# GpSimd's order of issue in a mixture-of-experts stage: the scatter of the tile two back ahead of the gather of the tile three ahead

## The reference

```python
# layer 0: 8 experts, top 2, hidden width 512
router_logits = x_flat @ moe_router
topk_logits, topk_idx = jax.lax.top_k(router_logits, 2)
topk_weights = softmax(topk_logits)
...
w13_out = jax.lax.ragged_dot(x_sort, moe_w13, group_sizes)
gate, up = jnp.split(w13_out, [512], axis=-1)
out_dispatch = jax.lax.ragged_dot(silu(gate) * up, moe_w2, group_sizes)
out_flat = zeros.at[token_ids_sort].add(out_dispatch * w_sort[:, None])
...
# layer 1: 16 experts, top 4 (of 2 groups out of 4), hidden width 256
for e in range(E):
    we = jnp.sum(weights * (indices == e), axis=-1)
    h = jax.nn.silu(x2 @ W1[e].T + b1[e]) * (x2 @ W3[e].T + b3[e])
    y = y + (h @ W2[e].T + b2[e]) * we[:, None]
...
# around them
x = x + tanh(g_xattn[0]) * xattn0(layernorm(x), ctx)
x = x + tanh(g_ffn[0])   * ffn0(layernorm(x))
x = x + tanh(g_xattn[1]) * xattn1(ctx, layernorm(x), mask)
x = x + tanh(g_ffn[1])   * ffn1(layernorm(x))
```

## Time and profile before

| | us |
|---|---|
| median of 3 runs | 2451.17 |
| lowest, highest | 2448.51, 2455.49 |
| the profiled execution, whole | 2443.97 |
| its span in the trace | 2442.2 |
| experts of layer 0, first gather to last scatter's start | 847.8 to 1190.0 |
| experts of layer 1, first gather to last scatter's start | 2023.3 to 2436.4 |
| PE busy over the span | 2078.9 (85%) |
| DVE busy | 1352.3 (55%) |
| POOL busy | 1291.8 (53%) |
| ACT busy | 929.8 (38%) |

### The profile page before, as it was taken

The page is one execution under the profiler, slowest core; times in us unless marked ns, Lnnn a source line. Parts: engine busy times, 40 slices in busy tenths (PEclk is TensorE's granted clock), DMA queues, the critical chain, the costliest instruction groups (busy, mean ns, idle before and its releaser), DMA issues. The chain is left out here.

```text
span 2442.2 us, 38632 instructions
## 1 busy us (share of the span) xinstructions
PE 2078.9 (85%) x10678; PEld 1354.3 (55%) x10678; DVE 1352.3 (55%) x4084; ACT 929.8 (38%) x2409; POOL 1291.8 (53%) x1552
## 2 busy tenths in 40 slices
PE   3988888888888499999578888888888857999997
PEld 3666666666666256666335555555555533555554
DVE  3666666666666211212247777777776743555554
ACT  1333333333333122222145655556555522333332
POOL 1333343433333234444247767777775744777777
PEclk9999999999999699999789999999998977999999
DMA  3101101010106022223201011011010535555554
GB/s 116 31 24 34 31 27 32 26 35 23 35 23 225 17 39 45 48 44 48 38 19 32 21 32 32 21 32 29 24 32 21 160 98 130 79 76 78 79 78 73
DMA packets 143793, 127.40 MB, mean 52 GB/s; under 512 B 48505, under 2 KB 134241, under 8 KB 143590
## 3 DMA queue, kind: packets, MB, share of 16 engines
q0 software_dynamic: 39456, 46.11, 11.8%
q1 hardware_dynamic: 96348, 70.67, 10.4%
q10 hardware_dynamic: 7786, 8.14, 1.0%
HBM read 87.16 MB, written 37.65 MB: 51 GB/s over the span
## 5 line engine op out<-in xcount | busy, mean ns | idle before, releaser
L1768 PE MATMUL psG<-expert_w,xgT 128*128 x688 | 329.3, 601 | 2.7 <-ACT xgT L1709 2.0
L549 ACT ACTIVATE prob<-psS,nm 100x361 f32<-100x361 f32 x256 | 141.4, 557 | 427.3 <-DVE nm L632 420.8
L777 POOL TENSOR_SCALAR prob<-prob,rc 100x363 f32<-100x363 f32 x256 | 160.4, 638 | 211.9 <-DVE rc L637 210.7
L1794 PE MATMUL psD<-expert_w,hT 128*128 x916 | 230.5, 384 | 2.8 <-ACT hT L1726 2.8
L1581 POOL DMA_INDIRECT xg<-xn,slots x178 | 175.6, 987 | 98.6 <-issue 50.9
L1594 POOL DMA_INDIRECT out<-y,slots x115 | 185.2, 1611 | 70.4 <-issue 25.9
L1709 ACT ACTIVATE xgT<-psX 128x256 f32<-128x256 f32 x172 | 66.0, 383 | 354.3 <-PE psX L1756 354.3
L1594 POOL DMA_INDIRECT acc<-y,slots x57 | 90.1, 1580 | 172.5 <-DVE y L1675 168.6
L971 PE MATMUL psJ<-wkv,cTn 96*121 96x512 f32 x384 | 181.2, 609 | 0.0
L1794 PEld LDWEIGHTS psD<-expert_w,hT 128*128 128x128 f32 x916 | 160.4, 190 | 21.4 <-issue 4.7
L1768 PEld LDWEIGHTS psG<-expert_w,xgT 128*128 128x128 f32 x688 | 118.8, 193 | 88.5 <-issue 88.5
(11 more groups left out here) (260 smaller groups left out, 4849.4 us busy)
## 6 DMA issues: line engine op xcount, KB each, us to landing
expert_w<-in_L_ffn_moe_w SPq DMA_DIRECT2D x8, 1024.0 KB
xn<-xm SPq DMA_DIRECT2D x64, 100.0 KB
bias<-in_L_ffn_b ACTq DMA_DIRECT2D x3, 2048.0 KB
ctx<-in_ctx SPq DMA_DIRECT2D x32, 181.5 KB
cT<-in_ctxT SPq DMA_DIRECT2D x32, 180.5 KB, 2.9
cT<-in_ctxT SPq DMA_DIRECT2D x64, 90.2 KB, 2.9
expert_w<-in_L_ffn_moe_w SPq DMA_DIRECT2D x8, 512.0 KB
expert_w<-in_L_ffn_W1T SPq DMA_DIRECT2D x16, 256.0 KB
```

The costliest lines, as they stand in the source:

```text
L549: s.activation(prob[:, q, 0:S], psS[0:N, h, 0:S], ACT.Exp, bias=nm[:, q:q + 1], accum_out=rs[:, q:q + 1]).then_inc(exp_done, 1)
L777: g.tensor_scalar(prob[:, q, :], prob[:, q, :], rc[:, q:q + 1], 1.0, ALU.mult, ALU.mult).then_inc(prob_done, 1)
L1768: mm = t.matmul(psG[:, r, :], xT[:, r, k, :], w13[:, bass.ds(e, 1), k, 0:512], start=k == 0, stop=k == 1)
L1794: mm = t.matmul(psD[:, r, 0:D], hT[:, r, k, :], w2[:, bass.ds(e, 1), k, :], start=k == 0, stop=k == KF - 1)
```

## The change

In POOL's loop the two calls change places. From iteration 2 on the scatter of tile j-2 is issued first and the gather of tile j+3 after it. Both expert stages run this loop. The three gathers ahead of it and the two scatters behind it stay, and so do all waits within the two calls.

```diff
                 gather(1)
                 gather(2)
                 for j in range(NT):
-                    gather(j + LOOK)
                     if j >= 2:
                         scatter(j - 2)
+                    gather(j + LOOK)
                 scatter(NT - 2)
                 scatter(NT - 1)
```

## The result

| | before | changed |
|---|---|---|
| median, us | 2453.33 (4 runs) | 2553.0 (4 runs, 2544.4 to 2562.1) |
| ratio to before | | 1.041, 95% interval 1.037 to 1.045 |
| profiled execution's span, us | 2442.2 | 2549.8 |

The change costs 4.1%, some 100 us, where the forecast was 86.5. A second measurement of the same kernel, beside three of the experiments, gave 2549.2 against 2447.8: 1.042 (1.040 to 1.044).

What follows compares the result with a forecast made beforehand. POOL's gather and scatter alternation was taken to bound layer 1's stage. Loop +78.2, boundaries +5.3, slow landings +2, start +1 and nothing for stage 0 made +86.5 on 2451.2: 2538 us, range 2517 to 2557.

Steps and rivals of the forecast that it cites:

- rival C: PE's clock falls to the lower level in layer 1's stage: 2552 to 2580 us, chance 0.12.
- the loop over two tiles: Layer 1: transposition, y, scatter, gather, transposition take 8.33 us within two tiles, 4.16 per tile, above POOL's 3.18.
- What bounds before, and what stays: Layer 1: POOL's alternation of gather and scatter sets the pace, 3.18 us per tile, and the alternation stays.
- transposition to y: Link in layer 1: y of tile k ends 2.81 us after the transposition of tile k+3 starts.
- y to scatter: Link from the end of y to the start of a scatter that waited for it: 0.78 us.
- boundaries: Layer 1, where a tile is the first of its expert: scatters must follow at 4.72, +5.3 us in all.
- gather to transposition: Link from a gather's start to the transposition that waits for it: 2.85 us, of which 2.80 to landing.
- slow landings: Layer 1: seven gathers land 0.3 to 1.0 us late, each pushing one of two loops: +2 us.
- Stage 0 at no cost: Layer 0's expert stage: PE-bound at 5.82 us per tile, about 3 us left for the gather, cost 0.
- start, end: Ends of layer 1's stage: scatter 3 starts later, +1 us; after scatter 111 nothing changes, 0.
- B, a shorter loop: Layer 1: a shorter y-to-scatter wait or ScalarE detour leaves about 3.90 us per tile: 2510 us, chance 0.12.
- D, not slower: Layer 1: POOL stays the bound if the path takes under 6.9 us instead of 8.33: 2450 us, chance 0.06.

Runs made afterwards that it cites:

- the filler: Changed kernel plus two unread 128x256 matmuls on PE per layer 1 iteration: 2549.06 us; again, 2546.61 against 2549.20 for the changed kernel.
- lead7: Kernel of before with look-ahead 4 instead of 3 and slot ring 16 instead of 8: 2443.58 us against 2449.15, ratio 0.998.
- swap_layer0: Kernel of before with the two calls changing places in layer 0's expert stage alone: 2446.57 us against 2446.73, ratio 1.000.

## Why the prediction was right, and where it was off

**The forecast and its range.** The measured 2553.0 lies in the range of 2517 to 2557, 15 above the forecast of 2538. It lies in rival C's 2552 to 2580 as well, so the time alone does not choose between them, nor does the sign that the prediction gave C, a granted clock under 1.00 between 2100 and 2500, which was seen. The traces choose: the loop over two tiles holds with the links forecast, and the runs with the filler cost the same at a granted clock of 1.00.

**What bounds before, and what stays.** Right. lead7 shows that look-ahead beyond six tiles is worth 0.2% at most and leaves the pace at POOL's, and the unchanged 0.98, 1.59 and 1.89 show that the alternation as such is the same.

**The loop.** Right, link by link. Over scatters 3 to 111 of the changed kernel the means are 2.91 from transposition to y (forecast 2.81), 0.93 from y to scatter (0.78, boundaries aside), 1.89 to the gather (1.89), 3.05 to the next transposition (2.85). Their sum 8.78 over two is 4.39, and 108 x 4.39 = 474.3, the 474.4 measured.

**The size, 102.8 for this stretch against 85.5.** The 17 us by the links, each as 54 times (108 tiles, two to a round of the loop) what it exceeds the forecast by:
- transposition to y, +0.10: 5.4 us. The shortest is 2.77, as before. POOL's gather now runs just while VectorE gets to yb and y, and y takes 0.40 on average with a gather beside it and 0.35 without. The gap between hid and yb tells less: 0.44 on average where a gather overlaps it (63 tiles), 0.35 where only a scatter does (23), but 0.41 where neither does (23). Whether the gather is a cause was not tested.
- y to scatter, +0.15: 8.2 us, of which the forecast had 5.3 as boundaries. 0.02 of it is the link itself, 0.80 and not 0.78 in nearly all tiles.
- gather to transposition, +0.20: 11.0 us, of which the forecast had 2 as slow landings. This is the term that was mis-sized, in two ways. Twelve gathers (tiles 14, 22, 28, 41, 49, 53, 68, 75, 89, 99, 102, 108) landed 0.4 to 1.5 later than the usual 2.80, 9.1 together, where the forecast took seven and 0.3 to 1.0; half of that, since each delays only one of the two loops that run side by side, is 4.6. And seven transpositions are late not for their gather but because PE's iteration before them took 4.67 to 6.02 us: tiles 15, 31, 42, 54, 60, 69, 79, as many as there are stretches at the lower clock there. They start 4.2 to 5.9 after their gather; over the usual 2.86 that is 12.8 together, and half of it, 6.4, is what the clock cost by this count. The forecast had the clock at nothing. In the first link it adds less than 1: the eight tiles that a stretch at the lower clock touches there have 3.07, the others 2.90.

One of them, in PE's order of time:

```profile
2210.78 0.69 PE L1756 MATMUL psX<-ident,xg 128*128 128x128 f32 x2 [2.93 <-DMA xg<-xn,slots]
...
2213.39 3.62 PE L1768 MATMUL psG<-expert_w,xgT 128*128 x4
2216.80 0.43 PE L1756 MATMUL psX<-ident,xg 128*128 128x128 f32 x2
```

A slow landing leaves PE idle for 2.93, after which the four matmuls of psG take 3.62 instead of 1.88, and tile 42 is transposed 6.02 after tile 41. The trace's granted clock falls to 0.5 (1.2 of 2.4 GHz) in such stretches, 27 us in seven. In all seven PE's iteration before had been stretched to 5.1 to 6.3 us by a wait; those that ended with tiles 28 and 44 were stretched as far (5.6 and 5.7), and the clock stayed at its upper level behind them. As a mean over the stage (changed kernel, then before):

```profile
2056.00:2520.00 464.00, 357.41 (x1267) 198.16 (x1266) 202.46 (x423) 114.05 (x316) 271.82 (x211) 0.97 0.39 61
```

```profile
2056.00:2440.00 384.00, 345.38 (x1304) 198.36 (x1302) 208.75 (x440) 123.45 (x326) 288.80 (x222) 0.99 0.51 78
```

**Boundaries, start, end.** In undisturbed stretches, such as scatters 57 to 61, spacings of 4.75 and 3.78 alternate where 4.72 and 3.60 were forecast; 2418.89 to 2423.64 above is one of the long ones. What stands before scatters beyond the 0.80 came out some 2 us dearer than the boundaries were counted; three such scatters (37, 73, 109) are no boundaries. They start 1.69 to 1.71 after their y, they stand 36 apart, and they are late by the same in the changed kernel's second trace; scatter 37 of layer 0 has 1.7 too, in the trace of before already. Together they make some 1.4 us of this; their cause is open. The start was right: scatter 3 stands 34.6 us behind the stage's first gather, 33.5 before, +1.1 for +1. The end cost 0.5 for 0.

**Stage 0 at no cost.** Right; swap_layer0 shows it, ratio 1.000.

**The rivals.** B, a shorter loop: fell. 0.80 from y to scatter in nearly every tile; the 0.29 is again seen at scatter 0 alone. C, the clock: it does fall, to 0.93 in one stretch of 100 us, as the comparison with 1900 to 2000 had it, but by the count above it costs some 6 to 7, not 14 to 40: PE at the lower level delays seven transpositions. The filler, with the clock at 1.00, saved 2.6 against the changed kernel beside it, within the noise; as it costs PE time itself, it sets no firm bound. D, not slower: fell by its own point, 6.9 us against 8.4 to 8.8 measured. By occupancy, which the Trainium skill's "Perfetto Trace Analysis" (section Identifying the Most-Contended Engine) would have one look at, no engine is fuller after than before: from 2200 to 2300 POOL falls from 76.0 to 56.4 of 100 us and PE from 92.8 to 77.6. The order of time shows what occupancy doesn't tell, a loop of waits through PE, ScalarE, VectorE, POOL and a DMA transfer.

**The landing time.** The changed kernel's gathers of the loop land 2.80 after their start in the median, 2.63 at the shortest. The fit in the Trainium skill's "DMA: Bandwidth & Descriptors" for a transfer issued by GpSimd (section on the anatomy of one DMA) gives an estimate of 2.30; the measurement decides.

## What to carry to other kernels

When the order of an in-order engine is changed, look at what stands behind each of its waits. Follow the path from the instruction that waits, over what its successor feeds, back to the same instruction some tiles later, and divide the path's latency by that number of tiles. The result is a pace like an engine's, and the largest pace sets the time. Here the same 8.5 us gave 8.7, 4.4 and, covered by POOL, 3.4 per tile at one, two and three tiles. A link changed by x then moves the time by x over that number per tile, which is also how an experiment tells the number.

## What the runs showed of the hardware

- A scatter that found its last wait unfulfilled started 0.78 us (layer 0) and 0.80 us (layer 1) after the end of the VectorE instruction that fulfilled it, in nearly all tiles, while the first scatter of a stage, whose only wait is that one, started 0.28 to 0.29 after. Scatters 37, 73 and 109 of layer 1 and 37 of layer 0 started 1.7 after it. Neither cause was tried.
- PE's granted clock fell at times to the lower level in the changed kernel's stage, with 76 to 78 of 100 us busy (0.93 to 1.00 by stretch), and stayed at the upper in the runs with the filler, with 91 to 94. Keeping it there by extra matmuls saved nothing that stands clear of the noise; they took 0.87 us of PE per tile.
- Two VectorE additions of 128x256 in a row, both of the same PSUM tile and without a dependency on each other, started 0.34 apart at 0.42 each.
